# One ring of three PSUM banks in place of two rings, a new step order and fewer waits on TensorE in a fused attention and feed-forward kernel

## The chip, the cores and the metric

The kernel runs on one core of one Trainium2 chip. The metric is the device time of the program in microseconds. The profile is of one execution of the same program. All engines named below belong to that one core: TensorE (PE, with its weight loads as PEld), VectorE (DVE), ScalarE (ACT), GpSimd (POOL) and SyncE (SP), which issues the DMAs.

## What is computed

The input is 16 sequences of 256 tokens with 128 features. A first part applies an adaptive layer norm and a linear attention and costs little. Then six layers follow on each sequence, and they take nearly all the time. Cut to what matters:

```
for i in range(6):
    x = attn_layer(shift_tokens(x), Wqkv[i], q_scale[i], k_scale[i], Wo[i]) + x
    x = ffn_layer(shift_tokens(x), ln_g[i], ln_b[i], W1[i], b1[i], W2[i], b2[i]) + x
# attn_layer: q, k, v for 16 heads of 64; q and k normalised per token and head,
#   rotated; attention in windows of 32 queries that see 64 keys; out @ Wo
# ffn_layer: layer norm, 128 -> 2 x 341, a * gelu(gate), 341 -> 128
```

All products are float32 except the ones with masks, selections and the split norm factors, which are bfloat16.

## The kernel before

One batch (one sequence of 256 tokens) in one layer is one unit of work, so there are 6 x 16 = 96 units. The units are software-pipelined. A function `walk` goes through periods, one for each unit, and in each period every engine runs its steps in an order that is written out by hand (`PE_ORDER`, `DVE_ORDER`, `ACT_ORDER`, `POOL_ORDER`, `SP_ORDER`). A step belongs to the current unit, to the next one (kinds in `AHEAD`) or to the one before (kinds in `BEHIND`). One period of TensorE is called a pass here.

The steps of TensorE, with their lines:

- PA0 to PA3 and PB0 to PB3 (L1236): projections to k (0, 1) and q (2, 3), for the next unit. DVE multiplies them with the rotary tables (RA, RB, L983), ACT squares them (QA, QB, L719), POOL adds the products (AD, L606).
- NK, NQ (L1247): sums of squares per head. CK, CQ on DVE clamp them, TK, TQ (L1255) turn them, RTK, RTQ on ACT make the reciprocal roots. POOL splits the k factors in three bfloat16 parts (RK). TU (L1263) turns these, UC on DVE copies them, KN0 and KN1 (L1272) spread them over the features, KM0 and KM1 on DVE (L999) multiply k with them.
- V0 to V3 (L1283): values for the next unit, copied by ACT (VC0, VC2) and DVE (VC1, VC3).
- S00 to S11 (L1291 the mask, L1301 the scores, 64 small products of 64x32 for each step): scores of two tiles of 128 queries in two halves. DVE takes the row maxima (M, L1016, L1021), ACT the exponentials (E00 to E13, L764).
- T00 to T11 (L1312): probabilities turned; DVE copies them out (TC, L1028). PV00 to PV11 (L1338, 64 small products each): probabilities times values; DVE scales them (AT, L1038). O00 to O11 (L1320): the result turned; ACT copies it out (OC, L752).
- WO (L1350), CEN (L1364), VAR (L1368), UP0 to UP2 (L1378), DN (L1385): output projection, layer norm and feed-forward of the unit before. BI works once in a layer.

SP moves q, k and v inside SBUF into the layout of the scores: MQ (8 DMAs), MK (8 DMAs) and MV (16 DMAs), all on one queue and in the order MQ, MK, MV.

PSUM has eight banks. Before, two of them form a ring (`RING`) for PA, PB, TU, KN and V; one, `turn_ps`, serves T, O and DN one after the other (`TURN`); two hold scores, two `out_ps`, one the norms. A step that takes a bank waits until its user before has been copied out:

```
RING = [s for s in PE_ORDER if s[0] in ("PA", "PB", "TU", "KN", "V")]
TURN = [s for s in PE_ORDER if s[0] in ("T", "O", "DN")]
```

Where a step has several waits, one sits on the instruction and the others stand in semaphore instructions ahead of it. `alone(pe)` puts the waits ahead of the scores, PV, TU and KN into a semaphore instruction of their own.

Of the kernel before, what the change touches and what calls it, by code (L numbers as in the profile page):

```python
# [113 lines left out]
RING = [s for s in PE_ORDER if s[0] in ("PA", "PB", "TU", "KN", "V")]  # L114
TURN = [s for s in PE_ORDER if s[0] in ("T", "O", "DN")]


def build(nc, t):

    with ExitStack() as ctx:  # L120
# [8 lines left out]
        ring_ps = [ctx.enter_context(nc.psum_tensor(f"ring_ps{i}", [P, 512], F32)) for i in range(2)]  # L129
        out_ps = [ctx.enter_context(nc.psum_tensor(f"out_ps{e}", [P, 512], F32)) for e in range(2)]  # L130
        turn_ps = ctx.enter_context(nc.psum_tensor("turn_ps", [P, 512], F32))
# [148 lines left out]
        end_ps = [bank[:, 0:TOKENS] for bank in (turn_ps, small_ps, *score_ps)]  # L280
# [123 lines left out]
        def bank_of(s, parity):  # L404

            return ring_ps[(parity * len(RING) + RING.index(s)) % 2]

# [205 lines left out]
        def _(act):  # L613
# [8 lines left out]
            nc.scalar.activation(wv_t[:, :], turn_ps[:, 0:DIM], ACT.Copy).then_inc(w_copied, 1)  # L622
            act.wait_ge(w_made, 1)
            nc.scalar.activation(v_ln[:, :], turn_ps[:, DIM:2 * DIM], ACT.Copy)
            nc.scalar.activation(bias_y[:, :], turn_ps[:, 2 * DIM:3 * DIM], ACT.Copy).then_inc(w_kept, 2)
# [10 lines left out]
            def first_step(kind, b):  # L636
# [63 lines left out]
                if kind == "KE":  # L700
                    act.wait_ge(f_kv, at(b, 1, 1))
                    act.wait_ge(f_kw, at(b, 1))
                    nc.scalar.activation(kv_t[:, :], turn_ps[:, 0:DIM], ACT.Copy, scale=float(TOKENS) ** -0.5
                                         ).then_inc(f_kvt, 1)
# [7 lines left out]
            def step(s, g, b, parity, layer):  # L712
                kind = s[0]
                if kind in ("QA", "QB"):
# [4 lines left out]
                    nc.scalar.activation(square[p % COUPLES][a][:, :], bank_of(("PB" if a else "PA", p), parity)[:, :],  # L719
                                         ACT.Square, bias=zero_col[:, :]).then_inc(sq_ready, 1)  # L720
                if kind == "VC":
# [3 lines left out]
                    nc.scalar.activation(vs[:, s[1] // 2, 0, :], bank_of(("V", s[1]), parity)[:, :], ACT.Copy  # L725
# [21 lines left out]
                if kind == "OC":  # L747
                    i, c = s[1], s[2]
                    act.wait_ge(o_made, at(g, 2 * TILES, 2 * i + c + 1))
                    if i == 0 and c == 0:  # L750
                        act.wait_ge(wo_ready, at(g, 1))
                    nc.scalar.activation(att_t[:, 4 * c:4 * c + 4, P * i:P * (i + 1)],  # L752
                                         turn_ps[:, :].rearrange("p (j c) -> p j c", c=P), ACT.Copy
# [714 lines left out]
```

## Time and profile before

| | us |
|---|---|
| median of 3 runs | 3772.42 (3762.76 to 3785.7) |
| the profiled execution, its own time | 3778.12 |
| the span of its profile | 3776.0 |

| engine | busy, us | share of the span |
|---|---|---|
| PE | 3505.9 | 93% |
| DVE | 2711.4 | 72% |
| ACT | 2723.8 | 72% |
| POOL | 1056.2 | 28% |

The page gives the busy time of an engine as the sum of its instructions. The end of a matmul is modelled, and one matmul overlaps the next, so a busy PE can still have short waits inside that share. They are read from the starts of successive groups in the timeline instead.

### The profile page before, as it was taken

What the parts mean: (1) busy time and instruction counts of PE and PEld (TensorE: products, weight loads), DVE (VectorE), ACT (ScalarE), POOL (GpSimd) and SP (SyncE); (2) the same over time, 40 slices, a digit from 0 to 9 for tenths busy, and PEclk for the clock granted to TensorE, in tenths of its full rate; (3) what the DMA queues carried; (4) which work ended last, traced back from release to release, by engine and by line L of the source; (5) the groups of instructions that cost most, each with busy time, mean ns of one, the idle gap of its engine ahead of it and who ended that gap; (6) DMA issues with size and microseconds to landing.
All of it is one profiled execution on the core that took longest, in us unless ns stands there. A gap on an engine that the chain in (4) does not pass through costs nothing.

```text
span 3776.0 us, 157290 instructions
## 1 busy us (share of the span) xinstructions
PE 3505.9 (93%) x64764; PEld 2470.2 (65%) x64764; DVE 2711.4 (72%) x5333; ACT 2723.8 (72%) x9033; POOL 1056.2 (28%) x892
## 2 busy tenths in 40 slices
PE   6789999999999999999999999999999999999997
PEld 4466666666666666666666666666666666666665
DVE  5667777777777777777777777777777777777774
ACT  5567777676767777776767777777768777777766
POOL 2222323332222233232332222232323232232320
PEclk9899999999999999999999999999999999999998
DMA  2065555645555555555454555555555555545453
GB/s 66 3 128 112 121 117 111 137 101 121 117 120 109 112 128 110 126 111 119 107 134 103 130 109 116 111 126 116 110 128 114 117 120 117 114 107 120 106 120 74
DMA packets 361291, 421.74 MB, mean 112 GB/s; under 512 B 52291, under 2 KB 265814, under 8 KB 359814
## 3 DMA queue, kind: packets, MB, share of 16 engines
q1 hardware_dynamic: 360582, 411.67, 50.4%
q8 instruction: 520, 8.52, 1.0%
q14 instruction: 189, 1.55, 0.1%
HBM read 19.30 MB, written 2.10 MB: 6 GB/s over the span
## 4 chain that ended last, share of the span: by engine, by line
PE 77%; ACT 13%; issue 4%; DVE 0%; SPq 0%; DMA 0%; POOL 0%; DVEq 0%; ACTq 0%
PE ring_ps L1236 19%; ACT probs L764 9%; PE out_ps L1350 9%; PE score_ps L1301 8%; PE out_ps L1378 7%; PE ring_ps L1283 7%; PE out_ps L1338 6%; PE turn_ps L1320 6%; PE turn_ps L1312 4%; PE small_ps L1247 4%; PE score_ps L1291 2%; ACT L746 2%; PE turn_ps L1385 2%; ACT att_t L752 2%; PE out_ps L1368 1%
## 5 line engine op out<-in xcount | busy, mean ns | idle before, releaser
L764 ACT ACTIVATE probs<-score_ps,neg_max,rq 128x64 f32<-128x64 f32 x3072 | 1200.4, 418 | 175.8 <-DVE neg_max L1021 174.5
L983 DVE TENSOR_TENSOR prod<-ring_ps,tables 128x512 f32<-128x512 f32 x1536 | 951.5, 682 | 155.2 <-PE ring_ps L1236 144.6
L606 POOL TENSOR_TENSOR ks<-prod 128x1024 f32<-128x1024 f32 x192 | 451.7, 2352 | 2106.2 <-DVE prod L983 2033.3
L1236 PE MATMUL ring_ps<-xs,wqk 128*128 128x256 f32 x3072 | 764.1, 387 | 11.7 <-ACT square L719 5.0
L719 ACT ACTIVATE square<-ring_ps,biases 128x512 f32<-128x512 f32 x768 | 508.8, 690 | 246.8 <-DVE prod L983 215.0
L764 ACT ACTIVATION_READ_ACCUMULATOR probs<-score_ps,neg_max,rq 128x1 f32 x3072 | 669.6, 218 | 0.0
L1236 PEld LDWEIGHTS ring_ps<-xs,wqk 128*128 128x128 f32 x3072 | 555.4, 191 | 114.7 <-issue 43.9
L752 ACT ACTIVATE att_t<-turn_ps 128x512 f32<-128x512 f32 x384 | 229.6, 598 | 493.0 <-PE turn_ps L1320 493.0
L606 POOL TENSOR_TENSOR qs<-prod 128x1024 f32<-128x1024 f32 x192 | 452.1, 2355 | 239.1 <-DVE prod L983 233.0
L1338 PE MATMUL out_ps<-v,pt 64*32 64x64 f32 x24576 | 348.4, 224 | 87.6 <-issue 86.4
L1283 PE MATMUL ring_ps<-wv,xs 128*128 128x512 f32 x768 | 406.6, 633 | 3.0 <-issue 2.9
L1338 PEld LDWEIGHTS out_ps<-v,pt 64*32 64x32 f32 x24576 | 276.6, 105 | 173.1 <-issue 173.0
L1038 DVE TENSOR_TENSOR att<-out_ps,inv_sums 128x512 f32<-128x512 f32 x384 | 247.5, 686 | 166.6 <-PE out_ps L1338 162.5
L1350 PE MATMUL out_ps<-att_t,wo 128*128 128x256 f32 x1536 | 349.6, 381 | 0.7 <-ACT att_t L752 0.7
L1320 PEld LDWEIGHTS turn_ps<-ident,att 128*128 128x128 f32 x1536 | 176.9, 145 | 229.7 <-ACT att_t L752 151.0
L1301 PEld LDWEIGHTS score_ps<-kt,qt 64*32 64x32 f32 x24576 | 263.5, 105 | 97.4 <-issue 96.7
L1350 PEld LDWEIGHTS out_ps<-att_t,wo 128*128 128x128 f32 x1536 | 292.4, 191 | 40.7 <-ACT att_t L752 0.9
L1320 PE MATMUL turn_ps<-ident,att 128*128 128x128 f32 x1536 | 254.0, 290 | 70.0 <-ACT att_t L752 66.8
L1028 DVE COPY pt<-turn_ps 128x512 f32<-128x512 f32 x384 | 262.6, 684 | 76.5 <-PE turn_ps L1312 76.0
L1301 PE MATMUL score_ps<-kt,qt 64*32 64x64 f32 x24576 | 299.4, 225 | 10.4 <-issue 8.9
L1378 PE MATMUL out_ps<-xg,w 128*128 128x256 f32 (+1 forms) x1152 | 298.6, 394 | 3.8 <-DVE xg L1064 3.3
L1016 DVE TENSOR_REDUCE row_max<-score_ps 128x8 f32<-128x512 f32 x384 | 246.5, 684 | 57.3 <-PE score_ps L1301 57.3
(184 smaller groups left out, 4291.6 us busy)
## 6 DMA issues: line engine op xcount, KB each, us to landing
v<-vs SPq DMA_DIRECT2D x1344, 128.0 KB
qt<-qs SPq DMA_DIRECT2D x768, 128.0 KB
kt<-ks SPq DMA_DIRECT2D x768, 128.0 KB
v<-vs SPq DMA_DIRECT2D x192, 64.0 KB
wqk<-in_L_ffn_Wqkv SPq DMA_DIRECT2D x6, 1024.0 KB, 5.2
wv<-in_L_ffn_Wqkv SPq DMA_DIRECT2D x6, 512.0 KB, 4.0
wo<-in_L_ffn_Wo SPq DMA_DIRECT2D x6, 512.0 KB
out_dram<-ks SPq DMA_DIRECT2D x16, 128.0 KB, 1.9
```

Of the source, the lines that this page charges most:

```text
L606: pool.tensor_tensor(dst, prod_a[p % 2], prod_b[p % 2], ALU.add).then_inc(rot_ready, 1)
L719: nc.scalar.activation(square[p % COUPLES][a][:, :], bank_of(("PB" if a else "PA", p), parity)[:, :], ACT.Square, bias=zero_col[:, :]).the ...
L752: nc.scalar.activation(att_t[:, 4 * c:4 * c + 4, P * i:P * (i + 1)], turn_ps[:, :].rearrange("p (j c) -> p j c", c=P), ACT.Copy).then_inc( ...
L764: last = nc.scalar.activation(probs[i][:, j, e, :], score_ps[e][:, KEYS * j:KEYS * (j + 1)], ACT.Exp, bias=neg_max[:, h:h + 1], scale=rq[p ...
L983: last = V.tensor_tensor((prod_b if a else prod_a)[p % 2][:, f, :] .rearrange("p (u c) -> p u c", u=2), bank[:, :].rearrange("p (u c) -> p ...
L1236: last = mm(bank_of(s, parity)[:, TOKENS * f:TOKENS * (f + 1)], wqk[:, n, 2 * c + f, a, :], xs[:, WINDOW:PADDED], start=True, stop=True)
L1283: mm(bank_of(s, parity)[:, :], xs[:, WINDOW + P * i:WINDOW + P * (i + 1)], heads[:, :, e, :], start=True, stop=True).then_inc(v_made, 1)
L1301: last = mm(score_ps[e][WINDOW * w:WINDOW * (w + 1), KEYS * j:KEYS * (j + 1)], qt[64 * e:64 * e + 64, j, q0:q0 + WINDOW], kt[64 * e:64 * e ...
L1320: last = pe.transpose(turn_ps[:, P * j:P * (j + 1)], att[i][:, 4 * c + j, :, :].rearrange("p e k -> p (e k)"), ident[:, :])
L1338: last = mm(out_ps[e][WINDOW * w:WINDOW * (w + 1), DIM_HEAD * j:DIM_HEAD * (j + 1)], pt[64 * e:64 * e + 64, j, WINDOW * w:WINDOW * (w + 1) ...
L1350: last = mm(out_ps[0][:, 0:TOKENS], wo[layer % 2][:, j, :], att_t[:, j, :], start=(j == 0), stop=(j == PAIRS - 1))
L1378: last = mm(out_ps[c % 2][0:size, TOKENS * n:TOKENS * (n + 1)], w1[layer % 2][:, col:col + size], xg[:, :], start=True, stop=True)
```

## The change

`turn_ps` goes, and its bank becomes the third of the ring. The ring now serves PA, PB, TU, KN, V, T, O and DN, 24 users in a pass, so each step has the same bank in each pass. The orders of PE, DVE and ACT are written anew; those of POOL and SP stay. On PE: S00 and S01 come first, ahead of PA0; T00 moves to behind TU; KN0, NQ, V0, KN1 and V1 stand ahead of PV00; PV00 and PV01 stand together, and so do PV10 and PV11; DN moves from between PV00 and PV01 to between O01 and O10. The waits are cut and reordered: PA and PB wait for `xs` once, `alone(pe)` goes everywhere, the wait for q sits on the second mask product and that for k on the first score product, and T has its wait for the exponentials first and that for the bank second. No computation is added or removed.

```
 PE_ORDER = """
-PA0 PB0 S00 S01 PA1 PB1 BI WO PA2 PB2 CEN NK T00 VAR PA3 TK PB3 UP0 S10 S11 UP1 UP2 TU T01 NQ KN0 PV00 DN KN1
-PV01 TQ T10 V0 V1 T11 PV10 O00 PV11 V2 O01 V3 O10 O11
+S00 S01 PA0 PB0 PA1 BI WO PB1 PA2 CEN PB2 VAR NK PA3 UP0 TK PB3 S10 S11 UP1 UP2 TU T00 T01 KN0 NQ V0 KN1 V1 PV00
+PV01 T10 V2 TQ V3 T11 O00 PV10 PV11 O01 DN O10 O11
 """
 DVE_ORDER = """
-XS RA0 RB0 M0 RA1 RB1 BI XA XB RA2 RB2 CK XG TC00 RB3 RA3 H0 M1 H1 H2 UC TC01 CQ KM0 X KM1 TC10 AT0 TC11 VC1 AT1
-VC3
+XS M0 RB0 RA0 RA1 BI XA XB RB1 RA2 RB2 XG CK RA3 RB3 H0 M1 UC TC00 TC01 KM0 H1 H2 CQ KM1 VC1 TC10 AT0 VC3 TC11
+AT1 X
 """
 ACT_ORDER = """
-QA0 QB0 E00 QA1 QB1 E01 E02 SQ QA2 QB2 LN E03 RTK LG G0 QB3 QA3 G1 G2 LE E10 E11 E12 E13 VC0 RTQ OC00 OC01 VC2
+E00 E01 QA0 QB0 E02 QA1 SQ QB1 LN QA2 E03 RTK LG G0 QB3 QB2 QA3 G1 G2 LE E10 E11 VC0 E12 E13 VC2 RTQ OC00 OC01
 OC10 OC11
 """
-RING = [s for s in PE_ORDER if s[0] in ("PA", "PB", "TU", "KN", "V")]
-TURN = [s for s in PE_ORDER if s[0] in ("T", "O", "DN")]
+RING = [s for s in PE_ORDER if s[0] in ("PA", "PB", "TU", "KN", "V", "T", "O", "DN")]
+BANKS = 3
...
                 if kind in ("PA", "PB"):
-                    pe.wait_ge(xs_ready, at(g, 1, 1))
...
+                    if (p, a) == (0, 0):
+                        pe.wait_ge(xs_ready, at(g, 1, 1))
...
                 if kind == "KN":
-                    pe.wait_ge(rkt_ready, at(g, 1, 1))
+                    if c == 0:
+                        pe.wait_ge(rkt_ready, at(g, 1, 1))
                     bank_free(g, s)
-                    alone(pe)
...
                         for e in range(2):
+                            if e == 1 and i == 0:
+                                pe.wait_ge(q_moved, moved(g, 1))
...
                         pe.wait_ge(k_moved, moved(g, 1))
-                        pe.wait_ge(q_moved, moved(g, 1))
-                        alone(pe)
...
                 if kind == "T":
-                    turn_free(g, s)
                     pe.wait_ge(exp_ready, at(g, TILES * PARTS, PARTS * i + 2 * (c + 1)))
+                    bank_free(g, s)
...
                 if kind == "PV":
+                    if (i, half) == (0, 0):
+                        pe.wait_ge(hidden_ready, at(g, FCHUNKS))
+                        pe.wait_ge(v_moved, moved(g, 1, V_MOVES))
...
+                    if (i, half) == (1, 0):
+                        pe.wait_ge(att_ready, at(g, TILES, 1))
                     pe.wait_ge(t_copied, at(g, 2 * TILES, 2 * i + half + 1))
-                    alone(pe)
```

## Rows read from the trace of the kernel before

**Rows 1.** Page, part 1: busy us, share of the span, instructions of each engine.

```profile
PE 3505.9 (93%) x64764; PEld 2470.2 (65%) x64764; DVE 2711.4 (72%) x5333; ACT 2723.8 (72%) x9033; POOL 1056.2 (28%) x892
```

**Rows 2.** Timeline of PE: start us, busy us, group; output projection of an early unit.

```profile
277.25 3.62 PE L1350 MATMUL out_ps<-att_t,wo 128*128 128x256 f32 x16
```

**Rows 3.** The same, 90 units later.

```profile
3603.11 3.62 PE L1350 MATMUL out_ps<-att_t,wo 128*128 128x256 f32 x16
```

**Rows 4.** Timeline of PE over one pass, bracket: idle before and its releaser.

```profile
1525.19 0.66 PE L1320 MATMUL turn_ps<-ident,att 128*128 128x128 f32 x4 [0.69 <-ACT att_t L752]
1525.68 1.89 PE L1236 MATMUL ring_ps<-xs,wqk 128*128 128x256 f32 x8
1527.41 0.59 PE L1291 MATMUL score_ps<-mask_bf,ident_bf 128*128 128x512 bf16 x2
1527.93 1.59 PE L1301 MATMUL score_ps<-kt,qt 64*32 64x64 f32 x128
...
1552.13 1.88 PE L1283 MATMUL ring_ps<-wv,xs 128*128 128x512 f32 x4
1554.27 0.63 PE L1312 MATMUL turn_ps<-ident,probs 128*128 128x128 f32 x4 [0.26 <-ACT probs L764]
...
1556.27 0.86 PE L1338 MATMUL out_ps<-v,pt 64*32 64x64 f32 x64
...
1558.02 0.60 PE L1320 MATMUL turn_ps<-ident,att 128*128 128x128 f32 x4
1558.45 1.02 PE L1283 MATMUL ring_ps<-wv,xs 128*128 128x512 f32 x2
1559.31 0.65 PE L1320 MATMUL turn_ps<-ident,att 128*128 128x128 f32 x4
1560.65 0.66 PE L1320 MATMUL turn_ps<-ident,att 128*128 128x128 f32 x4 [0.69 <-ACT att_t L752]
```

**Rows 5.** Waits of PE, 1000 to 2000 us: total us, times, longest.

```profile
PE out_ps L1338 <- issue: 26.3, 29, 2.6
PE turn_ps L1320 <- ACT att_t L752: 18.6, 27, 0.7
PE score_ps L1301 <- issue: 3.7, 5, 1.7
```

**Rows 6.** Timeline of PE around one long stall, in PV11.

```profile
1817.61 0.45 PE L1338 MATMUL out_ps<-v,pt 64*32 64x64 f32 x30
1820.65 0.51 PE L1338 MATMUL out_ps<-v,pt 64*32 64x64 f32 x34 [2.59 <-issue]
```

**Rows 7.** Page, part 3: packets, MB, share of 16 engines.

```profile
q8 instruction: 520, 8.52, 1.0%
```

**Rows 8.** Timeline of ACT in the pass of rows 4.

```profile
1531.72 0.41 ACT L764 ACTIVATE probs<-score_ps,neg_max,rq 128x64 f32<-128x64 f32 x1 [1.77 <-DVE neg_max L1021]
...
1538.18 1.27 ACT L719 ACTIVATE square<-ring_ps,biases 128x512 f32<-128x512 f32 x2
...
1547.79 0.41 ACT L764 ACTIVATE probs<-score_ps,neg_max,rq 128x64 f32<-128x64 f32 x1
...
1553.96 0.66 ACT L725 ACTIVATE vs<-ring_ps 128x512 f32<-128x512 f32 x1
```

**Rows 9.** Timeline of DVE in the same pass.

```profile
1526.74 2.48 DVE L983 TENSOR_TENSOR prod<-ring_ps,tables 128x512 f32<-128x512 f32 x4 [1.51 <-PE ring_ps L1236]
1529.73 1.29 DVE L1016 TENSOR_REDUCE row_max<-score_ps 128x8 f32<-128x512 f32 x2 [0.50 <-PE score_ps L1301]
...
1557.23 1.29 DVE L1038 TENSOR_TENSOR att<-out_ps,inv_sums 128x512 f32<-128x512 f32 x2 [0.85 <-PE out_ps L1338]
```

**Rows 10.** Timeline of POOL in the same pass.

```profile
1543.95 2.35 POOL L606 TENSOR_TENSOR qs<-prod 128x1024 f32<-128x1024 f32 x1
```

**Rows 11.** Timeline of the DMA queue of SP in the same pass.

```profile
1546.40 6.05 SPq L475 DMA_DIRECT2D qt<-qs  x8
1552.57 6.07 SPq L475 DMA_DIRECT2D kt<-ks  x8
```

More of the change, by code:

```diff
@@ L128, in build @@
         score_ps = [ctx.enter_context(nc.psum_tensor(f"score_ps{e}", [P, 512], F32)) for e in range(2)]
-        ring_ps = [ctx.enter_context(nc.psum_tensor(f"ring_ps{i}", [P, 512], F32)) for i in range(2)]
+        ring_ps = [ctx.enter_context(nc.psum_tensor(f"ring_ps{i}", [P, 512], F32)) for i in range(BANKS)]
         out_ps = [ctx.enter_context(nc.psum_tensor(f"out_ps{e}", [P, 512], F32)) for e in range(2)]
-        turn_ps = ctx.enter_context(nc.psum_tensor("turn_ps", [P, 512], F32))
         small_ps = ctx.enter_context(nc.psum_tensor("small_ps", [P, 512], F32))
@@ L279, in build @@
         x_fin, x_out = ([x[:, TOKENS * i:TOKENS * (i + 1)] for i in range(4)] for x in staged)
-        end_ps = [bank[:, 0:TOKENS] for bank in (turn_ps, small_ps, *score_ps)]
+        end_ps = [bank[:, 0:TOKENS] for bank in (ring_ps[2], small_ps, *score_ps)]
         mod_a = carve(P, BATCH, 6)
@@ L980, in step @@
                     dve.wait_ge(rot_ready, at(g, 2 * COUPLES, max(p - 1, 0)))
-                    bank = bank_of(pe_step, parity)
+                    bank = bank_of(pe_step)
                     for f in range(2):
@@ L998, in step @@
                         k_ = ks[:, a, 2 * c:2 * c + 2, :].rearrange("p u c -> p (u c)")
-                        last = V.tensor_tensor(k_, k_, bank_of(("KN", c), parity)[:, :], ALU.mult)
+                        last = V.tensor_tensor(k_, k_, bank_of(("KN", c))[:, :], ALU.mult)
                     last.then_inc(kn_ready, 1)
@@ L1164, in first_step @@
                     for tile in range(TILES):
-                        last = mm(turn_ps[:, 0:1], k_sq2[:, tile, :], qk_inv[i][:, tile, 1:2], start=(tile == 0),
+                        last = mm(ring_ps[2][:, 0:1], k_sq2[:, tile, :], qk_inv[i][:, tile, 1:2], start=(tile == 0),
                                   stop=(tile == TILES - 1))
@@ L1170, in first_step @@
                     for tile in range(TILES):
-                        last = mm(turn_ps[:, 0:DIM], v_tok[:, tile, :], qk_sq[i][:, tile, 1, :], start=(tile == 0),
+                        last = mm(ring_ps[2][:, 0:DIM], v_tok[:, tile, :], qk_sq[i][:, tile, 1, :], start=(tile == 0),
                                   stop=(tile == TILES - 1))
@@ L1183, in first_step @@
                     pe.wait_ge(f_kvt, at(b, 1, 1))
-                    mm(turn_ps[:, 0:DIM], kv_t[:, :], w_ln[:, :], start=True, stop=True).then_inc(f_kw, 1)
+                    mm(ring_ps[2][:, 0:DIM], kv_t[:, :], w_ln[:, :], start=True, stop=True).then_inc(f_kw, 1)
                 if kind == "Y":
@@ L1381, in step @@
                 if kind == "DN":
+                    bank_free(g, s)
                     pe.wait_ge(hidden_ready, at(g, FCHUNKS, FCHUNKS))
-                    turn_free(g, s)
                     for c, size in enumerate(FSIZE):
-                        last = mm(turn_ps[:, 0:TOKENS], w2[layer % 2][0:size, c, :], hidden[0:size, c, :], start=(c == 0),
+                        last = mm(bank_of(s)[:, 0:TOKENS], w2[layer % 2][0:size, c, :], hidden[0:size, c, :], start=(c == 0),
                                   stop=(c == FCHUNKS - 1))
```

82 lines of the change are left out of this document (36 added, 46 removed).

## The prediction

> **What bounds the kernel now.** I read the page first: TensorE is busy 93% of the span, ACT and DVE 72% each, POOL 28% [rows 1]. The work between the short stages at both ends is 96 equal passes. Two output projections that lie 90 units apart start at 277.25 and 3603.11 [rows 2, 3], so a pass takes 3325.86 / 90 = 36.95 us on average. So 0.5% of the time is 19 us or 0.2 us in a pass; that is about what a measurement of this kernel can tell from no change.
>
> Next I took one pass in the timeline of PE, from O11 to O11: 1560.65 - 1525.19 = 35.46 us [rows 4]. Its only named idle times are 0.69 ahead of O11 and 0.26 ahead of T11, so it is a clean pass, and the average pass is 1.49 us longer. The waits of PE say where that comes from. In 1000 us, which is 27 passes, 26.3 us of idle time "issue" lie inside the products of PV and 3.7 inside the scores, with no semaphore behind them, and 18.6 us ahead of O11 behind an ACT copy [rows 5]. So there are two kinds of loss, and the change must be judged on each.
>
> First, waits for other engines. They are read from starts, since the modelled ends hide part of them. From V3 to O10 a V step takes 1559.31 - 1558.45 = 0.86 us, and O01 takes 1558.45 - 1558.02 = 0.43 [rows 4]. V0 and V1 should thus take 1.72 and T11 starts 2.14 after them: 0.42 lost, behind the last exponentials. O10 should take 0.43 and O11 starts 1.34 after it: 0.91 lost, because O11 needs the one bank that O10 filled, and an ACT copy of 0.6 stands between. This one comes in each pass: 27 times in 27 [rows 5].
>
> Second, stalls of the instruction stream. In one PV11, 30 products run, then nothing for 2.59 us, then the other 34 [rows 6]. The instruction queue moved 520 packets of 8.52 MB / 520 = 16 KB [rows 7]; TensorE executed 64764 loads and as many products [rows 1], so a packet holds about 249 of them. PV00 with PV01 is 256 such instructions, one packet's worth. A packet's worth of projections would take 125 x 0.216 = 27 us, one of small products 1.6. My reading is that the stall is a packet that was not there yet. The Trainium skill (Advanced Engine Details and Errata, ISA Cache) gives the same size, a line of 16 KB for 256 instructions, and 128 KB in all on TensorE; by that room alone eight lines could be held and no stall of this kind would be due, but the trace has the stall of 2.59 us.
>
> **The change, part by part.** The products stay the same. I count from the clean pass of 35.46.
>
> The third bank for O and T. In the new ring O11 takes the bank that O01 had, and O01 lies DN and O10 ahead of it: six products at 1.73 / 8 = 0.216 [rows 4], so 1.30, and 0.43. The ACT copy of 0.6 ends long before. The 0.91 goes. DN covers the next one too: O10 needs AT1, which starts 0.1 after the end of PV11 (1557.23 against 1556.27 + 0.86) and takes 1.29 [rows 4, 9], so 1.39, and O01 with DN take 1.73. Without DN there, 0.96 of wait would come back.
>
> T11 behind E13. With S00 first, let its mask start at 0; the scores start at 0.52 [rows 4]. In the old pass E00 starts 1531.72 - 1527.93 = 3.79 after them [rows 4, 8], so now at 4.3. From E00 to the end of E13 ACT took 1553.96 - 1531.72 = 22.24 [rows 8]; the new order puts QA0 and QB0 between (two squares, 1.27) and VC0 (0.66), so E13 ends near 4.3 + 24.2 = 28.5. What PE still has to do from T11 to the end of the pass is T11 and four O steps at 0.43, 2.15, PV10 and PV11 1.6 (0.86 busy each, overlapping [rows 4]), DN 1.30 and changes of tile form 0.3, together 5.35; in a pass of 34.25 it reaches T11 at 28.9. The 0.42 goes, with 0.4 to spare. If ACT is late by more, T11 waits again and ACT becomes the bound of this part.
>
> Changes between large and small tiles. The two mask products should take 2 x 0.216 = 0.43, and the scores start 0.52 after them [rows 4]: 0.09 for going to small tiles. Four separate PV steps become two pairs, but KN0 and KN1 no longer stand against PV. Net two changes fewer, 0.18. I take 0.18; the bounds are 0 and 0.4. The Trainium skill (TensorEngine Tiling, Key Properties) has the engine drained at each change of tiling mode, not at a change of tile; the scores, with eight tile positions and one mode, agree, since they show the 0.09 only at their start.
>
> New waits. PB2 takes the bank of PA1 and so waits for QA1. ACT from 4.3: E00 and E01 (16 pairs of E took 1553.96 - 1547.79 = 6.17 [rows 8], so 3.09), QA0 and QB0 1.2, E02 1.54, QA1 0.6: 10.7. PE gets there at S 2.0, PA0 PB0 PA1 2.7, WO 3.45, PB1 PA2 1.73, CEN 0.43: 10.3. That is a wait of 0 to 0.4, and I take 0.2. O00 needs AT0, which DVE reaches behind KM1, VC1 and TC10; by my walk it ends within 0.1 of PE. I take 0.1. PA1 and PB1, KN, V1, T10 and V2 have over 0.3 to spare in the same walk; TC11 for PV11 has 0.1.
>
> The moves. RB3 ends about 1.24 (half of 2.48 [rows 9]) after PB3, at 17.2; POOL adds for 2.35 [rows 10], MQ and MK are issued in 1558.64 - 1546.40 = 12.24 [rows 11], so k is issued at 31.9. The scores of the next unit start at 34.25 + 0.52 = 34.8, 2.9 later. In the old pass that distance is 1563.39 - 1558.64 = 4.75 (the scores one pass on) and nothing waits. So the landing costs between nothing and 4.75 - 2.9 = 1.85; I take nothing, since a wait on the q and k moves shows nowhere in PE's waits [rows 5].
>
> The prologue and the last unit change by a step or two; I take 0. The removed semaphore instructions lie beside products and I cost them at 0 in the clean pass.
>
> Sum: 35.46 - 0.91 - 0.42 - 0.18 + 0.30 = 34.25, a gain of 1.2 in a clean pass.
>
> Stalls. Now 1.49. What speaks for more: PV00 and PV01 now run without a break, and so do PV10 and PV11, so a packet is used up in 1.6 us where DN, KN1 or O00 stood between. Scores in one piece of 256 stalled only 5 times in 27 passes, PV 29 times [rows 5], so length alone is not it; the old PV steps stand among waits in front of T11, PV and O, and S10 follows long products. S00 now follows PV, O and DN closely, so one dense run follows the other. What speaks for less: most waits now sit on loads and not ahead of them, so the sequencer may run on and ask for its next packet earlier. Bounds: 0.4 (as rare as in the scores, for three pairs) and 3.2 (each pass has one of 2.6 as in [rows 6] and a short one). I take 1.7, close to what is there.
>
> The pass: 34.25 + 1.7 = 35.95, 1.0 less than 36.95. Over 96 passes 96 us: span 3776 - 96 = 3680, execution 3682. The profiled execution (3778) lies 6 above the median of the runs, so the median comes to 3676.
>
> **Rivals.** (A) The forecast: waits go, stalls stay about as they are; 3620 to 3725. Chance 0.5. (B) The packets take the gain: with stalls over 1.49 + 1.2 = 2.7 in a pass the change turns slower; at 3.2 the pass is 37.45 and the time 3772 + 48 = 3820, at 2.7 it is 3772. For it: the doubled dense runs, the 2.59 stall. Against: the scores. Chance 0.2, of which 0.12 is slower by over 0.5%, 0.05 the same and 0.03 a small gain. (C) Moving waits onto the loads frees the stream and stalls fall to 0.5: pass 34.75, 2.2 less, 3772 - 211 = 3561, or so. Chance 0.12. (D) Waits come back in other places: k lands late for S00, or T11 and PB2 wait for ACT. ACT's chain from S00 to E13 has 0.4 to spare and the landing at most 1.85 too little; a wait of 0.7 in a pass leaves 96 - 67 = 29 us, 3743. For it: four tight places. Against: each came out at 0.2 or less by rows. Chance 0.18, of which 0.05 is the same, and nothing slower unless the whole 1.85 comes.
>
> **The numbers.** Faster 0.5 + 0.03 + 0.12 + 0.13 = 0.78; the same 0.10; slower 0.12. The range leaves out the slow end of B and half of C: 3580 to 3765.
>
> **What would show it.** Right: no idle time ahead of O11 and T11; waits of PE named after ACT under 0.3 in a pass; clean passes of 34.0 to 34.5; idle "issue" at PV near 1.7 in a pass. B: long issue stalls inside PV11 and S00, two in a pass. C: few of them. D: PE waits behind DMA at the scores or behind ACT at T11 or PB2. The prediction would be wrong above all where the stalls of the instruction stream don't stay near 1.5, since I have bounds for them and no law.

## The result and the profile after

The changed kernel takes 3636.14 us (median of four runs, 3633.57 to 3637.85) against 3779.06 before (3762.76 to 3786.36): ratio 0.9627, 95% interval 0.9591 to 0.9663. The forecast was 3676, 40 us more. The profiled execution of the changed kernel has a span of 3631.4 us. Its page, part 1 (answers to [rows 1]) and part 3 (answers to [rows 7]):

```profile
PE 3440.9 (95%) x64764; PEld 2500.4 (69%) x64764; DVE 2676.7 (74%) x5333; ACT 2701.4 (74%) x9033; POOL 1059.2 (29%) x892
...
q8 instruction: 512, 8.39, 1.0%
```

Loads and products are as many as before, and eight packets of instructions fewer were fetched. The timeline of PE shows the output projection of the second unit and that of 90 units later; they answer to [rows 2, 3]. The average pass takes (3467.53 - 272.06) / 90 = 35.51 us, against 36.95.

```profile
272.06 3.62 PE L1341 MATMUL out_ps<-att_t,wo 128*128 128x256 f32 x16
...
3467.53 1.68 PE L1341 MATMUL out_ps<-att_t,wo 128*128 128x256 f32 x7
```

One clean pass in the timeline of PE (start, busy, group; it answers to [rows 4]):

```profile
1584.38 3.62 PE L1341 MATMUL out_ps<-att_t,wo 128*128 128x256 f32 x16
...
1589.99 1.11 PE L1231 MATMUL ring_ps<-xs,wqk 128*128 128x256 f32 x4
1590.94 0.59 PE L1359 MATMUL out_ps<-xc_sq,mean_ones 128*128 128x256 f32 x2
...
1607.34 1.02 PE L1276 MATMUL ring_ps<-wv,xs 128*128 128x512 f32 x2
1608.20 0.60 PE L1305 MATMUL ring_ps<-ident,probs 128*128 128x128 f32 x4
1608.78 0.63 PE L1314 MATMUL ring_ps<-ident,att 128*128 128x128 f32 x4
1609.34 1.54 PE L1330 MATMUL out_ps<-v,pt 64*32 64x64 f32 x128
1610.81 0.66 PE L1314 MATMUL ring_ps<-ident,att 128*128 128x128 f32 x4
1611.30 1.46 PE L1377 MATMUL ring_ps<-hidden,w 128*128 128x256 f32 x6
1612.60 1.04 PE L1314 MATMUL ring_ps<-ident,att 128*128 128x128 f32 x8
1613.48 0.59 PE L1286 MATMUL score_ps<-mask_bf,ident_bf 128*128 128x512 bf16 x2
1614.00 1.73 PE L1294 MATMUL score_ps<-kt,qt 64*32 64x64 f32 x128
1615.66 2.86 PE L1231 MATMUL ring_ps<-xs,wqk 128*128 128x256 f32 x12
1618.36 0.81 PE L1341 MATMUL out_ps<-att_t,wo 128*128 128x256 f32 x3
```

From WO to WO it is 33.98 us, where before it was 35.46 from O11 to O11. O10 and O11 are now one row, which starts at 1612.60 and lasts 0.88 us to the next start, with no wait inside; T11 starts 0.86 us after V3 (1607.34 to 1608.20), the length of a V step. The waits of PE from 1000 to 2000 us, 28 passes (they answer to [rows 5]):

```profile
PE score_ps L1294 <- issue: 8.3, 5, 3.6
PE out_ps L1330 <- issue: 7.5, 4, 2.3
PE score_ps L1294 <- DMA kt<-ks: 5.0, 8, 1.5
PE ring_ps L1231 <- issue: 4.2, 2, 2.1
PE ring_ps L1314 <- issue: 2.7, 2, 2.4
PE ring_ps L1377 <- issue: 1.3, 1, 1.3
PE ring_ps L1276 <- issue: 0.5, 1, 0.5
```

The 18.6 us behind ACT are gone and no wait is named after ACT or DVE. Idle time "issue" sums to 24.5 us in 28 passes, where PV and scores alone had 30.0 in 27. New is a wait of 5.0 for the k moves, 0.18 us in a pass.

Four things below are read from the same traces by counting, and no single row shows them.

- A **border** is where TensorE's stream (loads, products and semaphore instructions, in the order of their records) passes from one 256 to the next. The named gaps over 0.8 us lie, all but single ones, at one place modulo 256 of the stream, in the kernels before and after and in the experiments that have many of them. Some of the traces lack one record in each pair of mask products, and the count allows for it.
- The **excess** of a kernel is its average pass less its short passes. It holds the stalls, what waits of some passes are left, and the slower clock that the next paragraphs describe.
- A semaphore instruction is called **held** where its record starts within 60 ns behind the update that it waits for, or, if the record is a long one, ends right behind it. Its wait was then still open when its turn came.
- The granted clock is read from its own records in the trace.

**The clock falls behind stalls.** The granted clock is at the 2.4 GHz level nearly everywhere. It falls to the 1.2 GHz level 11 times in the 90 passes of the changed kernel, and each of these falls stands behind a stall of 1.9 to 3.6 us. In the other kernels too, each fall in these passes stands behind a stall. The longest one of the changed kernel, in the timeline of PE and then by stretches (busy us, instructions, granted clock, DMA):

```profile
1511.41 0.44 PE L1294 MATMUL score_ps<-kt,qt 64*32 64x64 f32 x7 [3.63 <-issue]
1511.78 4.22 PE L1231 MATMUL ring_ps<-xs,wqk 128*128 128x256 f32 x12
1515.84 3.62 PE L1341 MATMUL out_ps<-att_t,wo 128*128 128x256 f32 x16
```

```profile
1506.00:1511.20 5.20, 1.78 (x123) 1.00 1.10 280
1511.20:1514.60 3.40, 3.19 (x14) 0.50 0.97 202
```

The 12 projections behind this stall take 1515.84 - 1511.78 = 4.06 us to the output projection. In the clean pass above they take 1618.36 - 1615.66 = 2.70. So this stall costs 1.36 us more than its idle time. At the lower level these products start 0.427 us apart instead of 0.216, so a microsecond there costs at most half a microsecond. The 90 passes spent 38 us at the lower level in the changed kernel and 44 in the one before, so this is at most 0.21 and 0.24 us of the excess of a pass. It is more where stalls are more, and the experiments give the number.

### The profile page after: what moved, and what is told of

Read it like the earlier page. It is cut to its first block, busy times and chain, and to the rows that moved or that the text cites. A ratio compares the mean times of both kernels' runs of the same rounds, so it can differ in the third digit from the quotient of the medians.

```text
span 3631.4 us, 155395 instructions
## 1 busy us (share of the span) xinstructions
PE 3440.9 (95%) x64764; PEld 2500.4 (69%) x64764; DVE 2676.7 (74%) x5333; ACT 2701.4 (74%) x9033; POOL 1059.2 (29%) x892
## 4 chain that ended last, share of the span: by engine, by line
PE 77%; SPq 8%; issue 4%; DMA 3%; POOL 1%; DVE 1%; ACT 1%; POOLq 0%; DVEq 0%; ACTq 0%
PE ring_ps L1231 19%; PE out_ps L1341 9%; SPq L475 8%; PE ring_ps L1276 7%; PE score_ps L1294 7%; PE out_ps L1370 6%; PE out_ps L1330 6%; PE small_ps L1242 5%; PE ring_ps L1314 4%; PE ring_ps L1305 4%; DMA kt<-ks 3%; PE ring_ps L1377 3%; PE score_ps L1286 2%; POOL qs L606 1%; PE ring_ps L1266 1%
## 5 line engine op out<-in xcount | busy, mean ns | idle before, releaser
L1231 PE MATMUL ring_ps<-xs,wqk 128*128 128x256 f32 x3072 | 776.4, 391 | 22.9 <-issue 14.8
L764 ACT ACTIVATION_READ_ACCUMULATOR probs<-score_ps,neg_max,rq 128x1 f32 x3072 | 699.9, 228 | 0.0
L752 ACT ACTIVATE att_t<-ring_ps 128x512 f32<-128x512 f32 x384 | 219.4, 596 | 375.1 <-PE ring_ps L1314 375.0
L1276 PE MATMUL ring_ps<-wv,xs 128*128 128x512 f32 x768 | 414.8, 622 | 0.6 <-issue 0.5
L1028 DVE COPY pt<-ring_ps 128x512 f32<-128x512 f32 x384 | 255.4, 686 | 125.3 <-PE ring_ps L1305 125.3
L1330 PE MATMUL out_ps<-v,pt 64*32 64x64 f32 x24576 | 311.6, 226 | 36.7 <-issue 34.9
L999 DVE TENSOR_TENSOR ks<-ks,ring_ps 128x512 f32<-128x512 f32 x384 | 244.3, 676 | 3.4 <-PE ring_ps L1266 3.4
L1314 PE MATMUL ring_ps<-ident,att 128*128 128x128 f32 x1536 | 229.9, 283 | 10.1 <-issue 8.8
```

What stands on the lines that cost most here:

```text
L764: last = nc.scalar.activation(probs[i][:, j, e, :], score_ps[e][:, KEYS * j:KEYS * (j + 1)], ACT.Exp, bias=neg_max[:, h:h + 1], scale=rq[p ...
L1231: last = mm(bank_of(s)[:, TOKENS * f:TOKENS * (f + 1)], wqk[:, n, 2 * c + f, a, :], xs[:, WINDOW:PADDED], start=True, stop=True)
L1276: mm(bank_of(s)[:, :], xs[:, WINDOW + P * i:WINDOW + P * (i + 1)], heads[:, :, e, :], start=True, stop=True).then_inc(v_made, 1)
L1314: last = pe.transpose(bank_of(s)[:, P * j:P * (j + 1)], att[i][:, 4 * c + j, :, :].rearrange("p e k -> p (e k)"), ident[:, :])
L1330: last = mm(out_ps[e][WINDOW * w:WINDOW * (w + 1), DIM_HEAD * j:DIM_HEAD * (j + 1)], pt[64 * e:64 * e + 64, j, WINDOW * w:WINDOW * (w + 1) ...
```

## The experiments

The changed kernel joins three things: the third bank of the ring, the new order of steps, and the new form of the waits. My sum put nearly all of the gain on bank and order. Each ratio is to the kernel before, timed on the same chip as the run (3785, 3774, 3772 and 3775 us in the four sets; 3779 in the result above). Where a time is set against the 3636 us of the changed kernel, the two are from different sets, and the difference is good to some 10 us. The difference of two ratios, times 3779, doesn't have this flaw, and it is given where it says something else.

**1. The new ring and order with the old waits.** The edit, at each place in this manner:

```diff
-                            if e == 1 and i == 0:
-                                pe.wait_ge(q_moved, moved(g, 1))
...
                         pe.wait_ge(k_moved, moved(g, 1))
+                        pe.wait_ge(q_moved, moved(g, 1))
+                        alone(pe)
```

> The ring of three banks and the new step order of the changed kernel, with the waits of TensorE as they were before (a wait on both moves and a lone semaphore instruction ahead of the scores and each PV step, waits on xs, xg, the turned norms and the attention rows repeated at each step). Theory: the waits that the change took away were all met long before, so they cost nothing in a clean pass; the pass without stalls stays at 34.0 to 34.2 us. They put about 19 instructions into a pass, which moves the places where the stalls of the instruction stream fall; since these places drift from pass to pass, their mean stays near 1.4 us. So 3636 us within 1% (3600 to 3670). Rival 1, the reordered waits themselves are worth something (the lone semaphore instruction ahead of PV and the scores drains TensorE or holds its loads back): each of the five places costs 0.1 us or more in each pass, 0.5 to 0.7 us, 3685 to 3705. Rival 2 (rival C of the prediction): moving the waits onto the loads is what kept the stalls down; with the old waits they grow back by 0.5 us or more in a pass, over 3685, and all of that lies in idle time named issue.

Measured: 3802.42 us, ratio 1.0042 (1.0023 to 1.0062), so 0.4% slower than before. Short passes are still 34.0 to 34.2 us, but the average one is 37.1: the excess is 3.0 us where the changed kernel has 1.5. (The profiled execution took 3780.55, the shortest of ten, so the typical one has some 0.2 more.) Waits of PE, 1000 to 2000 us:

```profile
PE out_ps L1332 <- issue: 32.6, 19, 2.5
PE score_ps L1295 <- issue: 17.3, 11, 2.8
```

and three borders of one pass in the timeline of PE, each a stall:

```profile
1598.91 0.70 PE L1277 MATMUL ring_ps<-wv,xs 128*128 128x512 f32 x1 [1.22 <-issue]
...
1604.51 0.35 PE L1332 MATMUL out_ps<-v,pt 64*32 64x64 f32 x16 [1.64 <-issue]
...
1610.57 0.64 PE L1295 MATMUL score_ps<-kt,qt 64*32 64x64 f32 x38 [1.46 <-issue]
```

My theory is refuted and the second rival holds: in a clean pass the waits are free, as expected, and yet their new form is worth 166 us (157 by the ratios). Nearly all of it is stalls of the instruction stream. At most 20 us are the clock that falls behind them: it was at the lower level for 79 us of the 90 passes, against 38.

**2. Only the ring; 3. the ring and the new waits.** Both with the old step orders on all engines (TensorE's shown).

```diff
 PE_ORDER = """
+PA0 PB0 S00 S01 PA1 PB1 BI WO PA2 PB2 CEN NK T00 VAR PA3 TK PB3 UP0 S10 S11 UP1 UP2 TU T01 NQ KN0 PV00 DN KN1
+PV01 TQ T10 V0 V1 T11 PV10 O00 PV11 V2 O01 V3 O10 O11
-S00 S01 PA0 PB0 PA1 BI WO PB1 PA2 CEN PB2 VAR NK PA3 UP0 TK PB3 S10 S11 UP1 UP2 TU T00 T01 KN0 NQ V0 KN1 V1 PV00
-PV01 T10 V2 TQ V3 T11 O00 PV10 PV11 O01 DN O10 O11
```

> Only the one ring of three banks, with the old step order of all engines and the old waits. By my account the third bank lets O11 start without waiting for the ACT copy of O10 (0.91 us in a pass), since three banks stand between them, but the old order has O10 straight ahead of O11 and the bank of O11 is then that of O01 (V3 and O10 lie between: 0.86 + 0.43 us, longer than the copy of 0.6). The 0.42 ahead of T11 stays (it is behind the exponentials), and new waits come in: in the old order DN stands between PV00 and KN1, and PA and PB follow each other. Theory: the bank alone brings about 0.7 to 0.9 us a pass, so 3690 to 3715. Rival 1: the order was what mattered, and the ring of three with the old order makes new waits as large as that it took away: 3740 to 3790. Rival 2: it is slower than before, since a ring step now waits for its user three steps back through slow users (O copies on ACT): over 3800.

> The one ring of three banks and the new waits, with the old step order. Against the kernel with the ring alone only the waits differ, so this is a second reading of what they are worth: theory 0 within 0.5% (a shift of the stalls only), so the same time as the ring alone; rival, waits that drain TensorE: 0.5 us a pass or more, 50 us less than the ring alone. Against the changed kernel only the order differs: theory, the order is worth the 0.42 ahead of T11 and 0.18 for two changes between large and small tiles and what new waits the old order has on the ring, so 50 to 80 us more than 3636.

Measured: the ring alone 3772.87 us, ratio 0.9967 (0.9953 to 0.9981); with the new waits 3686.74, ratio 0.9739 (0.9723 to 0.9756). Waits of PE, ring alone:

```profile
PE out_ps L1332 <- issue: 25.1, 27, 2.6
PE score_ps L1295 <- issue: 9.9, 8, 2.3
PE ring_ps L1314 <- ACT vs L725: 7.1, 23, 0.3
```

The 0.91 ahead of O11 is gone, but the old order makes O10 wait for the bank of V2, which ACT copies (7.1 us named; by the starts V3 to O10 is 1.34 where it was 0.86). Short passes are 34.94, 0.4 less than before. The excess rose by 0.5, to 2.1, and took nearly all of it. With the new waits short passes remain at 34.84 to 34.94 and the excess falls from 2.1 to 1.2. So the two ways of looking at the waits agree in kind (they act on stalls alone) and differ in size: 86 us in the old order, 166 in the new one. The order is worth 51 us with the new waits (42 by the ratios, where 50 to 80 were expected) and costs 30 with the old ones.

**4. DN back between PV00 and PV01.**

```diff
-PV01 T10 V2 TQ V3 T11 O00 PV10 PV11 O01 DN O10 O11
+DN PV01 T10 V2 TQ V3 T11 O00 PV10 PV11 O01 O10 O11
```

> The changed kernel with DN moved from its place between O01 and O10 back to between PV00 and PV01 (X on DVE moved along, to behind VC1). My prediction says: without DN between O01 and O10, 0.96 us of wait would come back, because O10 needs AT1, which starts 0.1 us after the end of PV11 and takes 1.29 us, and only O01 (0.43) is left to cover it. Theory: a wait of 0.9 to 1.0 us named after DVE stands ahead of O10 in each pass; clean pass 34.9 to 35.0, time 3636 + 90 = 3726 (3700 to 3745). Its time could be softened because a pause there lets the instruction stream catch up: then the stalls fall from 1.4 to 1.0 or so and the time is 3690. Rival: AT1 is early enough or the pair PV00, PV01 being split gives back as much; 3636 within 0.5%.

Measured: 3756.83 us, ratio 0.9919 (0.99 to 0.9938). Waits of PE:

```profile
PE ring_ps L1314 <- DVE att L1038: 25.7, 27, 1.1
PE out_ps L1330 <- issue: 14.6, 8, 2.2
```

25.7 / 27 = 0.95 us in a pass, where the prediction says 0.96. The time rose by 120 us (110 by the ratios), not 90, and lies outside the 3700 to 3745 that I expected: short passes are 35.1 to 35.2, 1.2 more than the 34.0 of the changed kernel. The other 0.2 is the cost of DN itself, which takes 1.50 from its start to PV01's between the small products (1000.45 to 1001.95 in the rows below) and 1.30 between O01 and O10 (1611.30 to 1612.60 above). The excess is the same as in the changed kernel, though its parts may differ: the clock was at the lower level for 106 us of the 90 passes, against 38.

```profile
1000.45 1.56 PE L1377 MATMUL ring_ps<-hidden,w 128*128 128x256 f32 x6
1001.95 0.86 PE L1330 MATMUL out_ps<-v,pt 64*32 64x64 f32 x64
```

**5 and 6. Which part of the old waits.** The lone semaphore instructions without the rest, and the rest without them.

```diff
                         pe.wait_ge(k_moved, moved(g, 1))
+                        alone(pe)
...
                     pe.wait_ge(t_copied, at(g, 2 * TILES, 2 * i + half + 1))
+                    alone(pe)
```

> The changed kernel with only the eight lone semaphore instructions of a pass put back (TensorE adds 1 to a counter ahead of TU, KN0, KN1, the scores of S00 and each of the four PV steps), the waits stay in their new form. The run with all old waits took 3802 us against 3636, and by its starts the whole loss lies in stalls (idle time named issue) in PV00, PV10, S00 and what follows them. Theory 1, the lone instruction is what costs: standing between a wait and a dense run of small products it keeps the sequencer from running ahead, so a block of 256 instructions is asked for later; then 3760 to 3810. Theory 2, the form of the waits costs (several waits ahead of a step make separate instructions): then the lone instructions alone leave 3636 to 3670. Each lone instruction is also one more instruction; by length alone that is 8 of 1351, 0.6 percent more blocks, nothing to be seen.

> The changed kernel with the old waits (on xs, xg, the turned norms and the attention rows at each step, both moves ahead of the scores) but without the eight lone semaphore instructions: the complement of the run before it. Theory 1 (the lone instruction costs): 3636 to 3670. Theory 2 (the form of the waits costs): 3760 to 3810. If both come out in between, the two add up or each wait and each lone instruction in the dense runs costs by itself.

Measured: 3782.38 us with the eight lone instructions (ratio 1.0025, 1.0009 to 1.0042), 3757.75 with the rest (0.9957, 0.9935 to 0.998). Each part costs most of the 166 by itself, 146 and 122 us, and together they cost hardly more. Short passes are 33.9 in both, so again it is the excess that grew, to 3.0 and 2.7 or so. Neither theory as I wrote it holds alone; both forms do it.

**7 and 8. The borders held at one place.** Semaphore increments that nobody waits for pad each pass to 1536 instructions; the two kernels differ by one number.

```diff
+            pads(32)
...
+                        pads(5)
```

> The changed kernel with 185 instructions that only add to a counter in each pass of TensorE, placed behind the long products (WO, PA, PB, V, UP, DN), so that a pass has 1536 = 6 x 256 instructions, and 32 of them ahead of everything. Theory: a stall comes where the stream passes from one block of 256 instructions to the next inside or soon after a dense run; in the changed kernel the border drifts by 71 from pass to pass, so about two of five borders fall badly. Here the borders stand at the same places in each pass: near the start of WO, and every 256 from there, which by the changed kernel's stalls are places that never stalled, as long as the padding itself doesn't move them into a dense run. So issue stalls fall from 1.4 us a pass to 0.3 or less; if the added instructions are free beside products of 0.216 us, the pass is 34.1 to 34.4 and the time 3500 to 3535 (faster than the changed kernel by 3 percent). Rivals: the added instructions cost 0.03 us each on TensorE: 185 x 0.03 = 5.5 us, time over 4100; or the stalls don't hang on the borders: 3636 or more.

> The same as the run with a lead of 32 but with a lead of 154 instructions in place of 32: the same work, the same 1536 instructions in each pass, and all borders 122 instructions earlier in the pass, so that one falls into the end of PV10 and PV11 and one into the scores of S00, where the changed kernel stalled for 2 and for 1.3 us, in each pass. Theory: the pass is 34.1 + 2.3 + 1.5 = 37.9 us, 3850 us, 300 us more than with a lead of 32, though the two kernels differ only by 122 instructions of the prologue. If the border doesn't matter, the two take the same time within 0.5 percent.

Measured: 4184.89 us (ratio 1.1088, 1.1065 to 1.1111) and 4479.77 (1.1866, 1.184 to 1.189). Both times missed what I expected, 3500 to 3535 and 3850, by over 600 us: the padding is anything but free, so neither kernel is of use. But the difference between them is 295 us, and 300 were expected. PE at the end of PV11 in two successive passes with the lead of 154 (the window begins inside the first row of each pass, so its count is not the whole step), and the same place with the lead of 32:

```profile
1439.83 1.35 PE L1339 MATMUL out_ps<-v,pt 64*32 64x64 f32 x90
1443.21 0.31 PE L1339 MATMUL out_ps<-v,pt 64*32 64x64 f32 x5 [2.03 <-issue]
...
1483.79 1.31 PE L1339 MATMUL out_ps<-v,pt 64*32 64x64 f32 x99
1486.83 0.31 PE L1339 MATMUL out_ps<-v,pt 64*32 64x64 f32 x5 [1.73 <-issue]
```

```profile
1506.28 1.67 PE L1339 MATMUL out_ps<-v,pt 64*32 64x64 f32 x128
1507.88 0.66 PE L1323 MATMUL ring_ps<-ident,att 128*128 128x128 f32 x4
```

The stall stands five products before the end of PV11 in 94 of the 96 passes, or never. Waits of PE at PV in 1000 us, lead 32 and then lead 154:

```profile
PE out_ps L1339 <- issue: 0.6, 2, 0.4
```

```profile
PE out_ps L1339 <- issue: 42.0, 22, 2.3
```

That the place of the border decides is shown by this. The price holds two things, the idle time and the clock behind it: with the lead of 154 the clock was at the lower level for 116 us of the 90 passes, at most 58 us of the difference, and with the lead of 32 never. What the padding cost is 7 us in a pass, nearly all between the scores and PA3: PE there waits for its stream, which spends 0.151 us on each increment (by the starts of successive ones). Later in the pass, three of the four V steps lost nothing with nine increments each.

**9. The same number of lone instructions elsewhere; 10. fewer waits still.**

```diff
                     last.then_inc(proj_ready, 1)
+                    if (p, a) in ((1, 1), (2, 0), (2, 1), (3, 0)):
+                        alone(pe)
+                        alone(pe)
```

```diff
-                    pe.wait_ge(exp_ready, at(g, TILES * PARTS, PARTS * i + 2 * (c + 1)))
+                    if not steady or (i, c) == (1, 1):
+                        pe.wait_ge(exp_ready, at(g, TILES * PARTS, PARTS * i + 2 * (c + 1)))
...
-                    bank_free(g, s)
-                    pe.wait_ge(hidden_ready, at(g, FCHUNKS, FCHUNKS))
+                    if not steady:
+                        bank_free(g, s)
+                        pe.wait_ge(hidden_ready, at(g, FCHUNKS, FCHUNKS))
```

> The changed kernel with eight lone semaphore instructions put back in each pass, as in the run that took 3782 us, but elsewhere: two each behind PB1, PA2, PB2 and PA3, beside products of 0.216 us and 10 to 20 us before the next dense run of PV products. In the padded runs such an instruction took 0.151 us in TensorE's stream of instructions, and beside long products TensorE's stream ran far enough ahead to hide it. Theory (the place decides: a lone instruction takes away the lead that the stream needs when a border of blocks comes within or behind small products): here the lead is won back before PV00, so 3636 to 3660. Rival (the number decides: 8 more instructions, or their shift of the borders from 71 to 79 a pass): 3760 to 3800, as with the eight in their old places.

> The changed kernel with more of TensorE's waits taken out, each of them covered by another wait that TensorE has met before it: the one of PA0 for the end of X (xs_ready comes later on DVE), of T00, T01 and T10 for their exponentials (the wait of S10, and the bank's wait for VC0), of PV00, PV01 and PV10 for the copied turns and the attention rows, and both of DN. The order of work and all products stay. By the places of the semaphore instructions in the trace of the changed kernel, about 6 of the 16 in a pass go, and 4 of these stand within or just ahead of dense runs. Theory: the eight lone instructions cost 146 us, 0.19 us each in a pass; six fewer of 0.15 us of the stream's time save 0.3 to 0.9 us a pass: 3550 to 3605, and all of the gain lies in idle time named issue. Rival: what is left of the stalls in the changed kernel is the wait for the block itself, which no lead shortens: 3636 within 0.5 percent. Second rival: TensorE gets ahead of the moves of k and waits for them more, over 0.4 us a pass, and the gain is half.

Measured: 3666.83 us (ratio 0.9744, 0.97 to 0.9789), so the eight cost 31 us beside the projections (44 by the ratios) and 146 in their old places; and 3640.24 (0.9649, 0.9619 to 0.968), no gain where I expected 30 to 85 us. Six semaphore instructions of a pass are gone in the second, 1345 instructions against 1351. Stalls are what they were, and so is the wait for k (4.9 us against 5.0). The number of these instructions and the stream's time that they take are thus not what counts. The waits that I took out had been met before. But one of the six instructions had been held: with the wait for the exponentials gone, the wait of T00 for an ACT square moved from a semaphore instruction onto the load. The held ones fell from 6.0 to 5.0 in a pass, and this brought nothing either.

**11 and 12. The eight, split by place.** Three ahead of TU, KN0 and KN1; five ahead of S00 and the PV steps.

```diff
                     bank_free(g, s)
+                    alone(pe)
                     turn = bank_of(s)[0:3 * HEADS, 0:TOKENS // 2].bitcast(BF16)
```

> The changed kernel with three of the eight lone semaphore instructions of a pass put back: those ahead of TU, KN0 and KN1, 15 to 19 us into the pass (counted from WO), that is before the two PV steps PV00 and PV01 and beside long products. What is known: all eight cost 146 us, eight beside the projections 6 to 10 us into the pass cost 31, and taking six more waits out brings nothing, so it is not the number and not a lead as such. With all eight, the border of blocks that falls into the end of PV0 or just behind it stalls in 38 of 46 passes where it falls there, in the changed kernel in 6 of 48, and the fetch for it starts 3 to 5 us after the border before, not 0.2 to 1.5. Theory P (what stands 1 to 4 us ahead of the dense run decides, because there the fetch for its border is asked for): most of the 146 us comes with these three, 3730 to 3780, all of the added stall in PV0 and the border after it. Theory Q (the lone instruction counts where it stands within or directly ahead of a dense run): 3636 to 3660.

> The complement: the changed kernel with the other five lone instructions put back, those directly ahead of S00, PV00, PV01, PV10 and PV11. Theory P: 3636 to 3680, the border in PV0 stalls about as seldom as in the changed kernel. Theory Q: 3730 to 3780. If both of these runs come out between, the costs add and no single place is the cause.

Measured: 3729.69 us (0.9869, 0.9835 to 0.9902) and 3687.38 (0.9766, 0.9737 to 0.9794): 94 and 51 us more than the changed kernel, together the 146 of all eight. Theory P had 3730 to 3780 and up to 3680, so it is met but for 7 us at the most. Three of them 1 to 5 us ahead of PV00 cost 31 us each, five directly ahead of small products 10 each, eight far away 4 to 6 each. In the three's kernel PE's waits and its semaphore instructions at this line (number, then shortest, median and longest in ns) are:

```profile
PE out_ps L1332 <- issue: 33.1, 21, 2.5
```

```profile
L415 PEldq EVENT_SEMAPHORE  x81: 51/51/625, 1018.1 to 1974.3; - x81
```

In the changed kernel the ones that hold a wait for ACT's squares are

```profile
L1206 PEldq EVENT_SEMAPHORE  x84: 51/51/51, 1029.4 to 1990.2; - x84
```

It is easy to read this as a wait that only the lone instruction carries, and as one for POOL's end of rk. The times don't bear it out. The lone instruction ahead of TU takes about 0.62 us in 95 of the 96 passes; one of them, and the last step of rk on POOL and the squares on ACT beside it:

```profile
L415 PEldq EVENT_SEMAPHORE  x1: 620/620/620, 1417.9 to 1417.9; - x1
1416.68 0.25 POOL L593 TENSOR_TENSOR rk_bf<-rk_rest,rk_bf 128x32 bf16<-128x32 f32 x1
1417.18 1.83 ACT L719 ACTIVATE square<-ring_ps,biases 128x512 f32<-128x512 f32 x3
```

POOL had ended at 1416.93, and over all passes the instruction ends 1.54 us behind that update, but 34 ns behind the update of an ACT square: the open wait is the one for the ring's bank. In the changed kernel a semaphore instruction of its own (L1206) waits for that square too, and it was held as well: the records at this place start 28 ns behind the update in 164 of 165 cases and then show 51 ns. A record of 51 ns thus doesn't say that nothing was waited for; only one that waits for two semaphores shows the time. The lone instruction ahead of KN0 is no different either, for there too a semaphore instruction was held before (L1208, 91 of 91). What the three really changed is KN1: its wait for a copy by DVE was on the load, and is now on the lone instruction, held in 87 passes of 88. The kernel has only one instruction more in a pass (1352 against 1351), since two of the three took the place of one that had stood there for a second wait. This points to one held instruction 2.5 us ahead of PV00 as what costs the 94 us, but no run has it alone.

The borders that fall into the end of PV01 and the steps behind it up to T11 stalled 37 times in 48, against 6 in 48 in the changed kernel.

## Why the prediction was right, and where not

The average pass came out at 35.51 us where 35.95 was forecast. Of these 0.44 us, 0.27 are the clean pass and 0.2 the excess, so 96 passes give the 40 us by which the forecast was too high.

**Waits that go: right.** Both named waits are gone, and the 0.96 of wait that DN covers is 0.95 in the run without it there. **The clean pass: 34.25 forecast, 33.98 measured.** The terms that were mis-sized: 0.2 for PB2 behind QA1 (PB2 takes 0.95 to VAR's start in the clean pass above against 0.86 of work, and on average 0.89, so 0.03 to 0.09), and the changes between large and small tiles, where DN's own move is worth 0.2 by the experiment and not 0.1. O00 behind AT0 is right: T11 to O00 is 0.58 for 0.43 of work.

**The moves: right in time, small in price.** I had k issued 2.9 us ahead of the scores (by its own terms the sum gives 31.8 and not 31.9, so 3.0). In the clean pass of the changed kernel the last k move is issued by 1610.81 and the scores start at 1614.00, 3.2:

```profile
1605.09 5.72 SPq L475 DMA_DIRECT2D kt<-ks  x8
```

I took nothing for the landing, bounds 0 and 1.85; it costs 5.0 / 28 = 0.18 in a pass, 17 us in all.

**Stalls: 1.7 forecast, 1.3 measured beside the landing, and by luck.** Of the 1.3, named idle time is 24.5 / 28 = 0.88 and the clock behind stalls at most 0.2; the prediction has no term for that clock. The two sentences that I put against each other were both right, and large. That two dense runs joined would use up a packet too fast (rival B, bound 3.2): with the old waits the new order has an excess of 3.0 and is slower than before, by 0.4%. That the waits now sit on loads and the sequencer runs on (rival C, 0.5): they take 1.5 us of that away. I had rated them as two small unknowns that about cancel, and gave the number by its nearness to the old one. That two terms of 1.5 us each did cancel is luck. The step that failed is "the removed semaphore instructions lie beside products and I cost them at 0 in the clean pass": true for the clean pass, while their part of the stalls was never priced. If ring, waits and order are changed one after the other, the runs give 12, 86 and 51 us. That is 149 against the kernel before of that set; the result itself has 143. If the order comes ahead of the waits, it is first a loss of 30, and the waits are worth 166.

A page bears on this. The Trainium skill (Perfetto Trace Analysis, Per-engine timelines) has a sequencer-only instruction wait within the sequencer, which fetches and decodes the next one only behind it, whereas a load or product is pushed into a wait queue and the sequencer goes on. The runs agree as far as they go: with the wait of KN1 on an instruction of the sequencer and not on the load, the kernel lost 94 us. They don't show it alone, since moving the wait of T00 the other way gained nothing. In ranking C at 0.12 I had this sentence's content as a guess and no number for it.

The same holds for the packet. The Trainium skill (Advanced Engine Details and Errata, ISA Cache) also says "Only 2 cache lines!" beside the 128 KB that I used. The traces side with two: on a stretch of small products the DMA for the next 256 starts about 1.3 us behind the border before, and where PE stalls it resumes 2.2 to 3.0 us behind that start (5th to 95th percentile of the stalls of the changed kernel, and about the same in the others). With room for eight packets, the one that is needed next would have been asked for long before. My estimate from these two numbers is that 256 instructions which are used up there in less than 3.5 to 4.3 us stall; PV10 with PV11 is 256 in 1.5 us.

**What stays open.** Why the fetch starts so late in the slow kernels. In the changed kernel the fetch for a border at the end of PV01 or just behind it starts at 0.9 us (median) behind the border before, with the eight lone instructions at 3.8, with the three at 2.8, and with the other old waits at 3.1. Held semaphore instructions are more in all of these: 6.0 in a pass in the changed kernel, 6.9 with the three, 9.3 with the eight, 12.8 with the other old waits. Between the end of the second scores and PV00 alone they are 3, 4, 5 and 7. So a held sequencer may be behind both forms of the old waits, but the count doesn't give the cost (94, 146 and 122 us), the ring alone has 11.3 at an excess of 2.1, and no run moves one held wait and nothing else. This would be the run to make next. A late block is also often followed by a second late one in the changed kernel (3 in 10 behind a stall of over 0.8 us, against 12 in 100 on the whole), while in the kernel before it isn't (4 in 48). Neither is explained.

No version beat the changed kernel; the one with six more waits out equals it.

## What to carry to other kernels

Where small products stand in long rows, look at the idle time with no releaser first: count TensorE's instructions between two such gaps, and if it is a multiple of 256, the place of each border is a term of the time and no wait on another engine will show it. Look at what waits stand in semaphore instructions of their own and are still open there, by the time of the update and not by the length of the record. Of several waits of a step the first one in the code went onto the load in this program, and the others into instructions ahead of it (TU's load carries the wait for rk, L1206 ahead of it the one for the bank). So a wait that may still be open should come first, and the ones that are surely met behind it. This is argued from the runs and not shown by one of its own. Taking out six instructions of a pass, five of them with waits met long before, brought nothing. Judge each part of a change in the surroundings in which it will run: here the new order cost 30 us under the old waits and gained 51 under the new ones.

## What the runs showed of the hardware

- A semaphore instruction takes 0.151 us of TensorE's stream each, by successive ones, where its own row says 51 ns. Some 100 of them between the scores and PA3 made the pass 7 us longer; beside three of the four V steps nine each cost nothing.
- At a border that stalls, PE stands still for 0.5 to 4.2 us, and moving all borders by 122 instructions changed a kernel by 295 us.
- Three semaphore instructions in a pass that add one instruction to the stream cost 94 us of 3636. One of them took an open wait off a load.
- A semaphore instruction with one open wait shows 51 ns in these traces and starts 28 ns behind the update (164 of 165 at L1206 in the changed kernel). One that waits for two semaphores shows time of its wait too, about 0.62 us ahead of TU.
- The granted clock, as the mean of a run, was 0.973 to 0.993 in all runs told of here. It is at the 2.4 GHz level but for short stretches at 1.2, and in the steady passes each of these stands behind a stall. They sum to 38 us of the changed kernel's 90 passes and to 79 with the old waits, where products of 128x256 start 0.427 us apart instead of 0.216.
